# One transformer block on one core: weights laid out block by block, the next row's input read at once, sums as bounds for two scales

## The reference

```python
xn = layernorm(x)
qkv = xn @ w_qkv.T + b_qkv                      # 16 heads of 32
attn = softmax(q @ k.T / sqrt(32) + causal) @ v
a = attn @ w_out.T + b_out
g = (xn @ gate_w.T) * gate_s                    # 1408 hidden, weights in -1, 0, 1
u = (xn @ up_w.T) * up_s
f = ((silu(g) * u) @ down_w.T) * down_s
out = x + a + f
```

## Time and profile before

| | us |
|---|---|
| median of 3 runs | 1996.45 |
| profiled execution, its own time | 1998.46 |
| its span | 1996.5 |
| PE busy | 1887.0 |
| DVE / ACT / POOL busy | 1349.7 / 1286.4 / 1356.9 |
| PE busy in 0 to 200 of the span | 117.7 |
| PE busy in 200 to 300 | 99.29 |

### The profile page before, as it was taken

How to read it: one execution, slowest core, us unless ns; L and a number is a source line. 1 busy time by engine, 2 the same in 40 slices (tenths; PEclk the granted TensorE clock), 3 DMA queues, 4 the chain that set the end, 5 groups by cost and what they waited for, 6 DMA issues and landing times.

```text
span 1996.5 us, 48141 instructions
## 1 busy us (share of the span) xinstructions
PE 1887.0 (95%) x15500; PEld 908.4 (45%) x15500; DVE 1349.7 (68%) x3908; ACT 1286.4 (64%) x2299; POOL 1356.9 (68%) x1094
## 2 busy tenths in 40 slices
PE   3676999999999999999999999999999999999995
PEld 1233444444444444444444444444444444444442
DVE  6885576766767676676767667676666767666663
ACT  2565676666766666676666667666676766667662
POOL 0157676787867668786766878676687866768664
PEclk9788999999999999999999999999999999999997
DMA  9145858777685877868687776868768696877865
GB/s 310 22 89 92 148 124 149 147 121 147 117 151 124 151 142 123 147 116 149 127 150 143 122 148 116 151 126 149 143 122 149 112 151 130 151 141 122 144 88 114
DMA packets 845569, 267.89 MB, mean 134 GB/s; under 512 B 817104, under 2 KB 817104, under 8 KB 845392
## 3 DMA queue, kind: packets, MB, share of 16 engines
q1 hardware_dynamic: 845392, 265.15, 71.2%
HBM read 46.94 MB, written 16.78 MB: 32 GB/s over the span
## 4 chain that ended last, share of the span: by engine, by line
PE 68%; POOL 10%; DVE 7%; issue 6%; SPq 5%; DMA 3%; ACT 1%; DVEq 0%; POOLq 0%; ACTq 0%
PE ps L461 68%; POOL phl L1098 4%; SPq L389 3%; POOL region_b L1076 2%; DMA p_t<-phl 2%; POOL memory L1093 1%; DVE memory L803 1%; DVE p L1006 1%; DVE part_max L784 1%; SPq L449 1%; SPq L447 1%; POOL region_a L1081 1%; POOL rstd L1072 1%; POOL o_hl L1103 1%; DVE hidden_tmp L941 1%
## 5 line engine op out<-in xcount | busy, mean ns | idle before, releaser
L461 PE MATMUL ps<-x_t,memory 128*128 128x512 f16 x4352 | 1003.2, 383 | 64.9 <-DVE memory L803 32.5
L1098 POOL TENSOR_TENSOR phl<-p,phl 128x1024 f16<-128x1024 f32 x320 | 683.7, 2136 | 422.8 <-ACT phl L742 407.8
L732 ACT ACTIVATE p<-p,nmax 128x384 f32<-128x384 f32 (+3 forms) x1024 | 529.9, 557 | 285.6 <-DVE nmax L1006 266.5
L461 PEld LDWEIGHTS ps<-x_t,memory 128*128 128x128 f16 x4352 | 405.9, 98 | 561.5 <-issue 108.0
L1006 DVE CUSTOM_DVE_ANT_0 p<-ps,causal,cst 128x384 f32<-128x384 f32 (+3 forms) x1024 | 515.3, 547 | 100.9 <-PE ps L461 79.5
L742 ACT CAST phl<-p 128x1024 f16<-128x1024 f32 x320 | 334.3, 1045 | 45.6 <-DMA p_t<-phl 27.6
L461 PE MATMUL ps<-memory 128*128 128x512 f16 x1408 | 322.2, 379 | 0.8 <-DVE bout_bc L874 0.8
L1093 POOL TENSOR_TENSOR memory<-hidden_tmp,memory 128x512 f16<-128x512 f32 x176 | 204.4, 1161 | 60.3 <-ACT memory L708 60.3
L461 PEld LDWEIGHTS ps<-vv,p_t 128*128 128x128 f16 x5120 | 187.6, 96 | 100.3 <-issue 27.8
L1014 DVE TENSOR_REDUCE ps<-ps 128x132 f32<-128x264 f32 (+1 forms) x320 | 122.1, 382 | 161.3 <-PE ps L461 160.9
L461 PE MATMUL ps<-vv,p_t 128*128 128x68 f16 (+1 forms) x5120 | 193.6, 185 | 20.6 <-DMA p_t<-phl 20.5
(11 more groups left out here) (61 smaller groups left out, 1297.5 us busy)
## 6 DMA issues: line engine op xcount, KB each, us to landing
region_b<-x SPq DMA_DIRECT2D x32, 1024.0 KB, 6.7
out<-region_b SPq DMA_DIRECT2D x64, 256.0 KB, 2.3
p_t<-phl SPq DMA_TRANSPOSE x640, 3.2
memory<-w_qkv_t SPq DMA_DIRECT2D x4, 768.0 KB, 7.6
memory<-gate_t SPq DMA_DIRECT2D x1, 2816.0 KB, 10.1
memory<-up_t SPq DMA_DIRECT2D x1, 2816.0 KB, 16.5
memory<-down_t SPq DMA_DIRECT2D x1, 2816.0 KB, 25.4
x_t<-region_a SPq DMA_TRANSPOSE x64, 4.1
```

What stands on the lines that cost most here:

```text
L461: return nc.tensor.matmul(o, lhsT=l, rhs=r, start=start, stop=stop, skip_group_check=True)
L732: last = nc.scalar.activation(cols, cols, ACT.Exp, scale=-1.0, bias=nmax[:, s % 2, i:i + 1])
L1098: g.tensor_tensor(phl[:, s % 2, 1, :], p32[:, s % 2, :], phl[:, s % 2, 0, :], ALU.subtract)\
```

## The change

Eight things are done, all ahead of the loop.

1. On the host the weights are laid out by blocks, so that each load is one contiguous run per partition (gate and up: runs of 4 KB). A block of gate or up is now one output tile with its four chunks, and the groups of gate and up take turns in `memory`. The three small vectors come as one array; the two broadcasts are issued last.
2. w_qkv comes as q, k, v, and each projection waits for its own splits only.
3. The low half of row 0's layernorm goes from DVE to POOL.
4. In the stage "none" DVE and ACT follow lists of their own (NONE_DVE, NONE_ACT): m are maxima of one group, h splits of gate and up.
5. The first four tiles of gate and up in row 0 multiply by the low half without asking the flag; so only g4 waits for it. The flag's maxima are taken in six parts (j) and three parts (e).
6. The bounds for w_out and down are sums of magnitudes, made by ACT with an accumulator (`sum_out`, t), in place of maxima made by DVE; the scale is multiplied by 2**-14.
7. Row 1's input is read at the start of row 0's period, not in slot 8, and its statistics, normalisation and low halves stand in earlier slots; SP's transposes of it in slot 13, not 15.
8. POOL_FIRST: the scale S0 and the flag F0 both lie in slot 2, the flag F1 in slot 10 (before: F0 in 1, S0 in 3, F1 in 8).

```diff
 DVE_FIRST = [
-    "| | | F0", "| a0 a1 | g0 |", "| u0 | c0 g1 |", "| u1 c1 | | g2 S0 u2", "| w0 | g3 | w1 w2 u3",
+    "h8 h9 | | j0 | j1", "h10 j2 | | h11 g0 j3 | j4", "j5 u0 F0 | | O0 |", "g1 | u1 | S0 | g2 u2",
...
 ACT_FIRST = [
-    "| | | |", "| | g0 | |", "u0 | | g1 | |", "u1 | | g2 | | w0 w1", "u2 g3 | | w2 | | w3", "g4 u3 w4 | | w5 | |",
+    "t0 h9 t1 h10 h11 | | | t2 t3 |", "g0 | | t4 | t5 t6 t7 |", "| g1 | u0 | |", "| | g2 | | w0 u1 w1",
...
+UNFLAGGED = 4
+NONE_DVE = ("m0 m1 q0 m2 m3 k0 m4 m5 v2 m6 v3 m7 m8 v0 m9 m10 v1 m11 M0 q1 X0 k1 h0 h1 q2 h2 h3 k2 h4 h5 q3 h6 k3 "
+            "h7").split()
+NONE_ACT = ("q0 k0 v2 v3 v0 v1 q1 k1 h0 h1 q2 h2 h3 k2 h4 h5 q3 h6 h7 k3 h8").split()
...
-            for c in range(DC):
-                first = FIRST_BLOCK[QKV] + 3 * c
-                sp.dma_start(float32_of(first, 3), w_qkv_t[c * P:(c + 1) * P, :]).then_inc(qkv_loaded[c], 16)
+            sp.dma_start(smalls_in[:, :], smalls).then_inc(smalls_loaded, 16)
+            for k in range(3):
+                load_run(float32_of(AT_BLOCK[QKV, DC * k], DC), w_qkv[:, k * DC * WB:(k + 1) * DC * WB], qkv_loaded[k])
...
             turn_x(0)
-            for i in (GATE, UP, OUT, DOWN):
-                load(i)
+            load_turned(GATE, gate, weights_loaded[GATE], gate_loaded_last)
+            load_turned(UP, up, weights_loaded[UP], up_loaded_last)
+            load_run(float32_of(AT_BLOCK[OUT, 0], DC), w_out, weights_loaded[OUT])
+            load_run(float32_of(AT_BLOCK[DOWN, 0], NT), down, weights_loaded[DOWN])
...
+                    if s == 0 and not prev:
+                        sp.wait_ge(sem["ln_lo"], at(b, "ln_lo", TT))
+                        sp.dma_start(x_in[:, :, :], x[b + 1].rearrange("(t p) n -> p t n", p=P))\
+                          .then_inc(sem["x_loaded"], 16)
...
-                    if s == 15 and nxt:
+                    if s == (15 if prev else 13) and nxt:
...
-            pe.wait_ge(w_lo_done, groups_until(QKV))
             for n, (kind, i) in enumerate(ITEMS["none"]):
+                pe.wait_ge(w_lo_done, ready_with(QKV, DC * "qkv".index(kind) + DC - 1))
...
-                        if mode == "first" and k == 0 and (kind, i) == ("g", 0):
-                            pe.wait_ge(w_lo_done, groups_until(UP))
+                        if mode == "first" and k == 0 and kind in "gu":
+                            pe.wait_ge(w_lo_done, ready_with(UP if kind == "u" else GATE, i))
+                        if mode == "first" and k == 0 and (kind, i) == ("g", UNFLAGGED):
                             pe.wait_ge(flags_done, 1)
                             has_lo["gate, up"] = pe.value_load(lo_flag[0:1, 0:1].bitcast(I32))
...
+            def sum_out(nth):
+                n = OUTS_GROUPS[nth]
+                i, block, count = GROUPS[n]
+                act.wait_ge(weights_loaded[i], 16)
+                if nth >= 2:
+                    act.wait_ge(outs_sums, nth - 1)
+                nc.scalar.activation(junk(nth)[:, 0:count * WB].rearrange("p (j n) -> p j n", n=WB),
+                                     float32_of(block, count).rearrange("p (j n) -> p j n", n=WB), ACT.Abs,
+                                     accum_out=group_max[:, n:n + 1]).then_inc(outs_sums, 1)
...
-            for t in range(TT):
-                dve.wait_ge(sem["ln_hi"], t + 1)
-                v.tensor_tensor(x_hl[:, t, 1, :], x_in[:, t, :], x_hl[:, t, 0, :], ALU.subtract)\
-                    .then_inc(sem["ln_lo"], 1)
...
             rstd_of(0)
+            for t in range(TT):
+                ln_lo(0, t)
+            pool.wait_ge(qkv_batch, 1)
             all_max(slice(0, 2), 1)
-            all_max(slice(2, 4), 3)
+            pool.wait_ge(ffn_in_batch, 2)
+            all_max(slice(2, 4), 2)
```

More of the change, by code:

```diff
@@ L200, with lay_group, groups_until, ready_with @@
 QKV, GATE, UP, OUT, DOWN = range(5)
-WIDTHS = [E3, FF, FF, D, D]
-CHUNKS = [DC, DC, DC, DC, NT]
+BLOCKS = [3 * DC, NT, NT, DC, NT]
 WB = 512
[L204 to L208, removed]
-MAX_COL = {QKV: 0, "hidden": 1, GATE: 2, UP: 3, OUT: 4, DOWN: 5, "bias": 6}
[L213 to L222, removed]
+LAG = 4
+GROUPS, AT_BLOCK = [], {}
+def lay_group(i, *blocks):
+    GROUPS.append((i, len(AT_BLOCK), len(blocks)))
+    for n in blocks:
+        AT_BLOCK[i, n] = len(AT_BLOCK)
+for n in range(0, 3 * DC, 2):
+    lay_group(QKV, n, n + 1)
+for n in range(0, NT, 2):
+    for i in (GATE, UP):
+        lay_group(i, *range(n, min(n + 2, NT)))
+for n in range(0, DC, 2):
+    lay_group(OUT, n, n + 1)
+for n in range(0, NT, 2):
+    lay_group(DOWN, *range(n, min(n + 2, NT)))
+GROUPS_OF = [[n for n, g in enumerate(GROUPS) if g[0] == i] for i in range(5)]
+OUTS_GROUPS = GROUPS_OF[OUT] + GROUPS_OF[DOWN]
+MAX_COL = {QKV: 0, "hidden": 1, GATE: 2, UP: 3, OUT: 4, DOWN: 5, "bias": 6}
+SMALLS = 3 * DC + 2 * NT
+UNFLAGGED = 4
+def groups_until(*kinds):
+    return max(max(GROUPS_OF[i]) for i in kinds) + 1
+def ready_with(i, n):
+    return max(k for k, (_, first, _) in enumerate(GROUPS) if first <= AT_BLOCK[i, n]) + 1
+NONE_DVE = ("m0 m1 q0 m2 m3 k0 m4 m5 v2 m6 v3 m7 m8 v0 m9 m10 v1 m11 M0 q1 X0 k1 h0 h1 q2 h2 h3 k2 h4 h5 q3 h6 k3 "
+            "h7").split()
+NONE_ACT = ("q0 k0 v2 v3 v0 v1 q1 k1 h0 h1 q2 h2 h3 k2 h4 h5 q3 h6 h7 k3 h8").split()
+def block_program(nc, x, w_qkv, gate, up, w_out, down, smalls, b_out, down_s, out):
     with ExitStack() as ctx:
@@ L287, in float32_of, with weight @@
             return area(2 * WB * (first_block + LAG), 2 * WB * n).bitcast(F32)
[L289 to L296, removed]
+        def weight(i, w, n, col, width):
+            start = 2 * WB * AT_BLOCK[i, n] + WB * w + col
+            return memory[:, start:start + width]
         def o_slot(i, n):
@@ L488, in ffn_part @@
                     last.then_inc(sem[name], 1)
-                else:
-                    with pe.If(has_lo["gate, up"] != 0):
-                        for c in range(DC):
-                            mm(ps[:, bank, :], weight(i, 1, c, cols), x_t[:, 0, c, :], False, False)
+                elif flagged:
+                    with pe.If(has_lo["gate, up"] != 0):
+                        low_half()
+                else:
+                    low_half()
             def down_part(b, bank, t, k):
@@ L503, in down_part @@
                 for i in tiles:
[L504 removed]
+                    last = mm(ps[:, bank, :], h_t(w, i, toks), weight(DOWN, 0, i, 0, D), k == 0 and i == 0,
                               k == 5 and i == NT - 1)
@@ L1160, with blocks, columns @@
     nc = bacc.Bacc("TRN2", target_bir_lowering=False, num_devices=1, dynamic_dma_scratch_size=2048)
-    arrays = {
-        "x": L0_attn_x, "w_qkv_t": np.asarray(L0_attn_w_qkv).T, "b_qkv": L0_attn_b_qkv,
-        "w_out_t": np.asarray(L0_attn_w_out).T, "b_out": L0_attn_b_out,
-        "gate_t": np.asarray(L0_ffn_gate_w).T, "up_t": np.asarray(L0_ffn_up_w).T,
-        "down_t": np.asarray(L0_ffn_down_w).T,
-        "gate_s": L0_ffn_gate_s, "up_s": L0_ffn_up_s, "down_s": L0_ffn_down_s,
+    def blocks(w_t, chunks, width):
+        rows, cols = w_t.shape
+        return w_t.reshape(rows // P // chunks, chunks, P, cols // width, width).transpose(2, 0, 3, 1, 4).reshape(P, -1)
+    def columns(v):
+        return np.asarray(v).reshape(-1, P).T
+    arrays = {
+        "x": L0_attn_x, "w_qkv": blocks(np.asarray(L0_attn_w_qkv).T, DC, D),
+        "gate": blocks(np.asarray(L0_ffn_gate_w).T, DC, P), "up": blocks(np.asarray(L0_ffn_up_w).T, DC, P),
+        "w_out": blocks(np.asarray(L0_attn_w_out).T, DC, D), "down": blocks(np.asarray(L0_ffn_down_w).T, 1, D),
+        "smalls": np.concatenate([columns(L0_attn_b_qkv), columns(L0_ffn_gate_s), columns(L0_ffn_up_s)], axis=1),
+        "b_out": L0_attn_b_out, "down_s": L0_ffn_down_s,
     }
```

274 lines of the change are left out of this document (154 added, 120 removed), and 11 rows, old and new, of tables (ACT_FIRST, DVE_FIRST).

## The result

The changed kernel took 2006.78 us, the median of 5 runs (2004.53 to 2009.29), beside 1996.54 for the kernel before on the same chip (5 runs, 1995.23 to 2000.42). The ratio is 1.0049 with a 95% interval of 1.0034 to 1.0064: 10 us slower, where 8.5 us faster was forecast, and outside the range. The profiled execution of the changed kernel is the slowest of its five, 2009.29 (span 2007.5).

What follows compares the result with a forecast made beforehand. The first 200 us bound the gain, with POOL full ahead of row 1's first projection: 202.5 - 193.0 - 1.0 = 8.5 us, so 1998.46 becomes 1990.0, and 1988.0 as median; range 1981 to 1994.5.

Steps and rivals of the forecast that it cites:

- The step that failed: From 200 us on: PE busy 99.29 of 100 us, so nothing to gain there, and the change leaves it untouched.
- the rivals: Besides D: the forecast, 5 to 11 us gained (0.50); POOL's idle time refilled, 13.5 (0.22); DVE-POOL clashes, 2.5 gained (0.19).
- D: Weight loads at the start: the new run shape moves half, 208 GB/s; 3.5 to 4.5 us slower, 2000.5; chance 0.09.
- p_lo(0): Row 0, after the row maximum and exponential: starts at 72.1 instead of 76.84, 4.7 us gained.
- Three trips: POOL's reductions over partitions in the first row: each costs 5.97 + 0.41 + 7.20 = 13.6 us; three before and after.
- p_lo(3): POOL, after both trips in slot 2: ends at 114.9 instead of 119.7, keeping the same 4.7 us.
- h_lo(10): Last hidden tile on POOL: ends at 175.8, 2.1 us gained, with 1.5 of 6.6 us idle time refilled.
- r0: First projection of row 1 on PE: starts about 193.0 without the 4.45 us wait, against an effective 202.5 before.
- New gaps: PE behind the start of row 1, values(15) being late next: 1.0 us taken off the gain (0 to 3.6).
- first scale unmoved: Start of row 0: DVE's 2.5 us saved are given back waiting for POOL's reduction, at 22.7; delay taken as 0.
- ACT's sum of 1024 elements: ACT's accumulating bounds for w_out and down: 1.15 us each; twice that would put p_lo(1) 4 us later.
- my own signs of failure: Up's maxima waiting for a load; POOL idle over 3 us beyond its reductions in slots 4 to 16; PE gaps behind r0.

Runs made afterwards that it cites:

- slot 186: Changed kernel with the head of PE's loop over rows 1 to 14 placed at slot 186 of a 256-instruction fetch block: 1989.80 us, ratio 0.9958.
- slot 170: Changed kernel with the head of PE's loop placed at slot 170 of its 256-instruction fetch block: 1989.38 us, ratio 0.9958.
- fewer waits: Changed kernel, no head placed, with 19 repeated PE waits for weight groups ahead of the loop left out: 1989.43 us, ratio 0.9958.
- both heads at 186: Adds the kernel before with its PE loop head placed at slot 186, 1996.39 us (0.9998), beside the changed kernel with the same head, 1989.80 us.
- the kernel before at 214: Kernel before with only the head of PE's loop placed at slot 214 of its fetch block: 2011.39 us, ratio 1.0072.
- A head at 200: Changed kernel with the head of PE's loop placed at slot 200 of its fetch block: 1994.69 us, ratio 0.9986.
- the flag asked for at tile 2: Changed kernel with PE's loop head at slot 186 and two instead of four gate and up tiles unasked (UNFLAGGED = 2): 1994.80 us, ratio 0.9998.

## Why the prediction was wrong

**The step that failed** is in its first paragraph: "that part has nothing to give and the change does not touch it (the sequences after the first keep their tables)". The tables were kept and the busy share was full, so the change had nothing to win there; but it could lose. The instructions that it adds ahead of the loop moved the loop's head within its fetch block, and each row then took 1.15 us more. Of these, 0.8 are the issue gap (9.5 / 12) and 0.2 the longer wait for p (5.3 less 2.6, in 12 rows); 0.1 is left without a wait that I can name. None of the rivals named it; D, the one that ended slower, was about the loads, and they were in time (380 GB/s in 20 to 30, 438 in 30 to 40). With that term away, at slot 186, slot 170 or with fewer waits, the same change gives 1989.8, 1989.4 and 1989.4, a ratio of 0.9958. The forecast was 1988.0.

**The first row**, term by term, at slot 186 with the kernel before in brackets. First matmul 27.42 (32.52). p_lo(0) 70.89, 6.0 us gained; the forecast was 4.7. Three trips, two in slot 2 and one in slot 10, with 5.8 to 6.2 us ahead of each reduction and 7.0 to 7.7 behind; I had taken 13.6 for one and they took 13.3 to 14.0. p_lo(3) ended at 114.6 (119.7), 5.1 us gained; forecast 4.7. h_lo(10) ended at 177.4 (177.9), 0.5 us gained where 2.1 were forecast, so POOL refilled none of its waits there (6.6 us of them, as before), and the term came out toward its lower end. r0 started at 194.77 at the full rate, forecast 193.0, against 202.5: 7.7. At the first milestone 215.33 - 208.57 = 6.8 us were left, and in the other runs of the changed kernel with the turn in slot 13 and four tiles unasked 6.2 to 7.6, but for the profiled execution of the kernel itself, where the two trips in slot 2 took 14.1 and 14.2 us, 0.5 and 0.9 longer, and 4.5 were left. "8.5 us gained" was 1 to 2 too much. New gaps of 0.66 behind r0 and 0.71 behind the first milestone make 1.4 where the sum had 1.0.

**Right by its own steps:** first scale unmoved (22.41 against 22.55), the DVE time given back by POOL's preparation; ACT's sum of 1024 elements, 1.04 with 0.19 for the accumulator's read at its end, 1.05 us from one start (71.12) to the next (72.17), where 1.15 was taken and not twice 1.14; no wait of up's maxima for a load; the wait for x and the slow matmuls behind it gone.

**Not seen beforehand**, because I read the loop only by its averages and took it for one even stretch. PE's added waits ahead of the loop were there to be seen in its order. I gave them no term, since each is satisfied when it is reached; their price is the room that they take. Of my own signs of failure two did not come: up's maxima waited for no load, and the one POOL wait over 3 us apart from the reductions (3.59 at 195.04) lay behind the tiles that set r0. The third, "if PE has gaps behind r0", did come, and it was right. But it does not show where I had looked: 200 to 300 has PE busy for 99.50 of 100 us, and the first issue gap is at 330.

## What to carry to other kernels

Where an engine runs a long loop at full load, count what a change adds or removes ahead of the loop on that engine, also instructions that wait for nothing. Read a row or two at the loop's head for "issue" gaps before and after. A placed head, or fewer redundant waits, tells such a loss from a true one: compare two kernels with the same head before judging either. Here that turned +0.49% into -0.42%, with both heads at 186 -0.40%.

## What the runs showed of the hardware that was not expected

- PE goes on with its next fetch block 2.5 to 3.3 us behind the loop's first matmul, at three head positions, and 1.2 to 1.5 us behind the end of the block's packet. With 28 instructions of the head's block left the gap was 2.1 us a round, and the time 38 us over that of the same kernel with the head at 186 (2028.07 against 1989.80).
- With the head at the first slot of a block, the gap is ahead of the head: 0.84 to 1.48 us, 15.0 us in 12 rounds.

```profile
PE ps L503 <- issue: 15.0, 12, 1.5
```

- The way out of the loop costs too: in the last row PE has an issue gap of 1.81 us in the changed kernel and 1.43 in the kernel before at 214.
- A head at 200 and one at 186 differ by 0.4 us a row with no issue gap in either. The DMA transpose of x that is issued just behind a 16 KB code packet takes 1.7 to 2.4 us in the mean of a profile's 12 rows in place of 1.2, and the place of the head decides which one that is.
- A reduction over partitions cost POOL 5.7 to 6.3 us ahead and 6.7 to 7.7 behind in each trip of slots 2 and 10, in nine profiles of the changed kernel and its variants (but for one way back, at the flag asked for at tile 2, that ended in a wait for ACT).
